# Layer 0 of a four-layer transformer kernel: attention scores by single heads in two row tiles of TensorE, low parts and rotary products on VectorE, and a step of unpacking moved forward

## What is computed

```python
xn = _layernorm(x, axis=-1)
x = x + _L0_attn_ref(xn, ...) + _L0_ffn_ref(xn, ...)
...                                             # layers 1, 2, 3 in the same form

# layer 0, attention: 32 heads of 16 columns
q, k, v = proj(wq), proj(wk), proj(wv)          # (4, 32, 256, 16)
q, k = _apply_rope(q, sin, cos), _apply_rope(k, sin, cos)
scores = einsum('bnth,bnsh->bnts', q, k) / sqrt(16)
scores = where(causal, scores, -inf)
out = einsum('bnts,bnsh->bnth', softmax(scores), v)

# layer 0, FFN: 4-bit weights, W[k, n] = scales[g_idx[k], n] * (w4[k, n] - (z4[g_idx[k], n] + 1))
out = (silu(xf @ Wg) * (xf @ Wu)) @ Wd          # 512 -> 1376 -> 512
```

## Time and profile before

| | |
|---|---|
| median of 3 runs | 2557.12 us (2554.77 to 2557.39) |
| profiled execution, its own time | 2561.34 us |
| span from its first to its last instruction | 2559.6 us |
| mean granted TensorE clock | 0.983 of full speed |
| busy: PE / PEld / DVE | 2455.2 / 1962.8 / 1618.1 us |
| busy: ACT / POOL | 1102.4 / 618.3 us |
| first scores matmul of `att0` to last values matmul | 337.6 to 480.3 us |

### The profile page before, as it was taken

How to read it: one execution, slowest core, us unless ns; L and a number is a source line. 1 busy time by engine, 2 the same in 40 slices (tenths; PEclk the granted TensorE clock), 3 DMA queues, 4 the chain that set the end, 5 groups by cost and what they waited for, 6 DMA issues and landing times. The chain is left out here.

```text
span 2559.6 us, 40914 instructions
## 1 busy us (share of the span) xinstructions
PE 2455.2 (96%) x14448; PEld 1962.8 (77%) x14448; DVE 1618.1 (63%) x2388; ACT 1102.4 (43%) x2158; POOL 618.3 (24%) x455
## 2 busy tenths in 40 slices
PE   5989999999989989999999999999999999999899
PEld 4767777778866668888888878888888877888666
DVE  5886567864477776545444467777777776543576
ACT  3322145443255533223333366666666653323453
POOL 3343110246321226124444400000000024430100
PEclk8999999999989999999999999999999999999999
DMA  2232164122332212234444332222222222322421
GB/s 86 62 101 83 52 122 88 31 38 43 57 89 59 48 28 42 45 98 140 148 148 143 125 114 87 83 90 90 68 75 86 66 44 39 53 46 33 102 63 37
DMA packets 406207, 195.33 MB, mean 76 GB/s; under 512 B 280393, under 2 KB 359729, under 8 KB 406079
## 3 DMA queue, kind: packets, MB, share of 16 engines
q1 hardware_dynamic: 404860, 191.53, 30.0%
q10 hardware_dynamic: 1218, 2.06, 0.3%
HBM read 129.85 MB, written 44.04 MB: 68 GB/s over the span
## 5 line engine op out<-in xcount | busy, mean ns | idle before, releaser
L603 PE MATMUL banks<-xn_hi,w_hi 128*128 128x512 f32 x1264 | 496.6, 393 | 12.9 <-ACT sgf L1146 10.0
L603 PE MATMUL banks<-xn_lo,w_hi 128*128 128x512 f32 x1264 | 493.1, 390 | 0.0
L603 PE MATMUL banks<-xn_hi,w_lo 128*128 128x512 f32 x1264 | 492.9, 390 | 0.0
L603 PEld LDWEIGHTS banks<-xn_hi,w_hi 128*128 128x128 f32 x1264 | 238.0, 188 | 64.4 <-DVE w_lo L591 10.4
L603 PEld LDWEIGHTS banks<-xn_hi,w_lo 128*128 128x128 f32 x1264 | 237.9, 188 | 49.7
L603 PEld LDWEIGHTS banks<-xn_lo,w_hi 128*128 128x128 f32 x1264 | 238.1, 188 | 48.4
L591 DVE TENSOR_TENSOR w_lo<-tw,w_hi 128x512 fp32r<-128x512 f32 (+2 forms) x136 | 117.0, 867 | 201.8 <-ACT w_hi L583 201.7
L2719 DVE TENSOR_SCALAR raw<-banks,cols 128x512 f32<-128x512 f32 x128 | 103.7, 810 | 180.3 <-ACT sq L2702 180.3
L2731 POOL TENSOR_TENSOR ssq<-ssq,sq 128x512 f32<-128x512 f32 x128 | 165.1, 1290 | 183.2 <-ACT sq L2702 183.2
L469 POOL TENSOR_TENSOR nat<-nat,wscale 128x512 f32<-128x512 f32 (+1 forms) x44 | 51.5, 1179 | 651.6 <-DMA nat<-in_L_ffn_w 651.4
L1258 POOL TENSOR_TENSOR h_lo<-sgf,h_hi 128x512 fp32r<-128x512 f32 (+1 forms) x94 | 128.1, 1367 | 288.8 <-ACT h_hi L1149 288.8
(11 more groups left out here) (302 smaller groups left out, 5831.5 us busy)
## 6 DMA issues: line engine op xcount, KB each, us to landing
qk_scratch<-raw SPq DMA_DIRECT2D x64, 512.0 KB, 3.0
qk_raw<-qk_scratch SPq DMA_DIRECT2D x64, 512.0 KB, 3.8
nat<-in_L_ffn_w SPq DMA_DIRECT2D x48, 256.0 KB
head_scratch<-stage SPq DMA_DIRECT2D x16, 512.0 KB, 3.2
st_qs<-st_hi SPq DMA_DIRECT2D x128, 64.0 KB, 2.1
nat<-in_L_attn_Wq SPq DMA_DIRECT2D x32, 256.0 KB
nat<-in_L_attn_Wk SPq DMA_DIRECT2D x32, 256.0 KB
nat<-in_L_attn_Wv SPq DMA_DIRECT2D x32, 256.0 KB
```

What stands on the lines that cost most here:

```text
L603: mm = nc.tensor.matmul(to[half][:, :], w[0:n, j, k * P:(k + 1) * P], r, start=first and k == 0 and x == 0, stop=last and k == len(rows) - ...
```

## The change

**Attention of layer 0.** A slot's 128 rows become two row tiles of 64, one for each head of a pair: rows 0 to 15, 16 to 31 and 48 to 63 of a tile hold the three terms of one head, rows 32 to 35 its four rows of maxima. Each head of a pair has matmuls of its own with 64 rows, in the row tile e = 0 or 1; a step holds heads of one row tile. `both` issues a step of scores and a step of shifted scores of the other row tile alternately. The masks come from two 64-row blocks (`square`, `row64`), so a step's mask is two bf16 matmuls. New functions `pe_att0`, `dve_att0`, `act_att0`, `sp_att0` stand beside the old ones, which layers 1 and 3 still use. Values are split in two halves with the transposes and two `both` between them. ACT copies the maxima in two instructions of 4 rows instead of one of 32. A unit takes 12 loads instead of 9 for the same bytes, and from the fourth on 2 more that clear the maxima rows. The cleared buffers are the queries (128 rows x 2048) instead of the keys (96 rows x 4096).

```diff
+        def score_heads(part):
+            return (0, part, 0, PAIRS) if part < 2 else (1, part % 2, 2 * (part // 2 - 1), 2)
+        def shift_heads(part):
+            return (0, part % 2, 2 * (part // 2), 2) if part < PAIRS else (1, part % 2, 0, PAIRS)
+        def pe_att0(pe, s):
+            def tile(e, width):
+                return slice(e * ROW_TILE, e * ROW_TILE + width)
+            def both(i, part, j, part2):
...
+                for b in range(2):
+                    if here:
+                        nc.tensor.matmul(o[:, :, qt * P + b * ROW_TILE:qt * P + (b + 1) * ROW_TILE], square[tile(e, ROW_TILE), 0, b, :],
+                                         bcast(row64[tile(e, ROW_TILE), :], n_p), start=b == 0, stop=False, skip_group_check=True)
+                    if there:
+                        nc.tensor.matmul(o2[:, :, b * ROW_TILE:(b + 1) * ROW_TILE], square[tile(e2, ROW_TILE), 1, b, :],
+                                         bcast(row64[tile(e2, ROW_TILE), :], n_p2), start=b == 0, stop=False, skip_group_check=True)
+                for x in range(PAIRS):
+                    if here and x < n_p:
+                        mm = nc.tensor.matmul(o[:, x, :], q[tile(e, ROW_TILE), p + x, qt * P:(qt + 1) * P], k[tile(e, ROW_TILE), p + x, 0:keys],
+                                              start=False, stop=x == n_p - 1, skip_group_check=True)
...
+                    if there and x < n_p2:
+                        mm = nc.tensor.matmul(o2[:, x, :], k2[tile(e2, ROW_TILE), p2_ + x, kb * P:(kb + 1) * P],
+                                              q2[tile(e2, ROW_TILE), p2_ + x, kb * P:SEQ],
+                                              start=False, stop=x == n_p2 - 1, skip_group_check=True)
...
+            for i in range(-3, CHUNKS):
+                for n in range(3):
+                    both(i + 2, 3 + n, i + 1, n)
+                values(i, 0, 0)
+                tops(i + 2)
+                for n in range(2):
+                    both(i + 3, n, i + 1, 3 + n)
+                values(i, 0, 1)
+                values(i, 1, 0)
+                values(i, 1, 1)
+                both(i + 3, 2, i + 1, 5)
...
+        def act_att0(act, s, wo):
+            def copy_tops(i, e):
...
+                rows = slice(e * ROW_TILE + QUAD, e * ROW_TILE + QUAD + PAIRS)
+                ins = nc.scalar.activation(att_queries(s, i)[rows, :, :], bcast(bank[5][rows, i % 2 * SEQ:(i % 2 + 1) * SEQ], PAIRS), ACT.Copy)
```

```diff
         def dve_low_x(dve, s, half):
-            for k in range(0, KT, 2):
-                low_x(dve, nc.vector, s, half, k)
+            for k in range(KT):
+                low_x(dve, s, half, k)
...
+                nc.vector.tensor_tensor(seqs(v), seqs(v), bcast(cst[:, C_COS0:C_COS0 + SEQ], 2), ALU.mult).then_inc(step_c.sem, 1)
                 nc.vector.tensor_tensor(seqs(rot), seqs(rot), bcast(cst[:, C_SIN0:C_SIN0 + SEQ], 2), ALU.mult)\
```

```diff
             ins.then_inc(dequant.sem, 1)
+            if i + 1 < s.n:
+                dve_unpack(dve, s, i + 1, (i + 1) % SLOTS, parts_of(s, i + 1))
+            dve_lo(dve, s, i, j, parts)
...
+            def down_ahead(left):
+                if left == 1:
+                    dve_unpack(dve, s.then, 0, 0, parts_of(s.then, 0))
+                    dve_dequant(dve, s.then, 0, 0, parts_of(s.then, 0))
```

More of the change, by code:

```diff
@@ L61 @@
 C_MASK = 384
+C_NEG1 = 512
 C_COS0, C_SIN0, C_COS1, C_SIN1 = 520, 776, 1032, 1288
@@ L98, in constants @@
     c[96 + np.arange(HPC), C_NEG + np.arange(HPC)] = -1.0
+    for e in range(2):
+        c[e * ROW_TILE + QUAD + np.arange(HPC // 2), C_NEG1 + np.arange(HPC // 2)] = -1.0
+    row, of, to = np.arange(P)[:, None] % ROW_TILE, np.arange(2)[None, :, None] * ROW_TILE, np.arange(P)[None, None, :]
+    for x, later in enumerate((of + row[:, :, None] > to, to > of + row[:, :, None])):
+        c[:, C_SQUARE + 2 * P * x:C_SQUARE + 2 * P * (x + 1)] = np.where(later, MASKED, 0.0).reshape(P, 2 * P)
+    c[:, C_SQUARE + 4 * P:] = row == np.arange(ROW_TILE)[None]
     for _, row, groups in TABLES:
@@ L1141, in ahead @@
                     pe_up_delta(pe, s, i, j, ft)
-            up_rounds(pe, s, ahead, work, opening, lead=LEAD - 1 if s.behind else LEAD_TURN, first=first, seam=seam_pe(pe, s))
+            def down_ahead(left):
+                if left == 1:
+                    pe_down_ahead(pe, s.then, 0)
+            up_rounds(pe, s, ahead, work, opening, lead=LEAD - 1 if s.behind else LEAD_TURN, first=first,
+                      seam=down_ahead if s.then else seam_pe(pe, s))
         def act_gate(act, s, half):
@@ L1248, in work, with down_ahead @@
                     dve_gated(dve, s, half)
-            up_rounds(dve, s, ahead, work, opening, LEAD if s.tw is None else LEAD_TURN, first, pair, 1, seam_dve(dve, s))
+            def down_ahead(left):
+                if left == 1:
+                    dve_unpack(dve, s.then, 0, 0, parts_of(s.then, 0))
+                    dve_dequant(dve, s.then, 0, 0, parts_of(s.then, 0))
+            up_rounds(dve, s, ahead, work, opening, LEAD if s.tw is None else LEAD_TURN, first, pair, 1,
+                      down_ahead if s.then else seam_dve(dve, s))
         def pool_up_scale(pool, s, i, j, ft):
@@ L1375, in proj_order @@
         def proj_order(s, ahead, work, opening, lead=LEAD, seam=None):
-            for i in range(min(lead, s.n)) if opening else ():
+            for i in range(1 if s.up and s.up.then is s else 0, min(lead, s.n)) if opening else ():
                 ahead(i, i % SLOTS, s.chunks[i])
@@ L1389, in load, with pe_down_ahead @@
             def load(i, j, c):
-                sp_slot(sp, s, i)
+                if s.up and s.up.then is s and i < SLOTS:
+                    sp.wait_ge(centred.sem, s.up.cen0 + s.up.n - (s.up.n - 1 - i) % SLOTS)
+                else:
+                    sp_slot(sp, s, i)
                 for dst, src in c["loads"]:
                     sp.dma_start(dst(j), src).then_inc(loaded[j].sem, 16)
+            if opening and s.up and s.up.then is s:
+                load(0, 0, s.chunks[0])
             proj_order(s, load, lambda i, j, c: None, opening, LEAD_LOAD)
+        def pe_down_ahead(pe, s, i):
+            c = s.chunks[i]
+            pe_spread(pe, s, i, i % SLOTS, [HOT["down"] + kt * P for kt in c["kts"]], c["cols"])
         def pe_chunk_delta(pe, s, i):
@@ L1402, in ahead @@
                 if s.mode == "dequant":
-                    pe_spread(pe, s, i, j, [HOT["down"] + kt * P for kt in c["kts"]], c["cols"])
+                    pe_down_ahead(pe, s, i)
                 elif s.adapters:
@@ L3287, in build @@
         down0 = plan_proj(packed_down_chunks(t["L0_ffn_down_qweight"], F0), "dequant", KT, h_of((h0_hi, h0_lo)), "dve", up0)
+        up0.then = down0
         v0 = plan_v0()
```

291 lines of the change are left out of this document (224 added, 67 removed).

## The result

| | before | after |
|---|---|---|
| median, runs made in turn | 2557.0 us | 2569.16 us |
| ratio, 95% interval | | 1.0045 [1.0034, 1.0056] |
| profiled execution, its own time / span | 2561.3 / 2559.6 | 2569.62 / 2567.8 us |
| first scores of `att0` | 337.6 | 330.0 |
| last values of `att0` | 480.3 | 492.7 |

The change is slower by 0.45%, against 2525 us forecast. By stages of the two profiled executions, the front gains 7.6 us, attention takes 162.7 instead of 142.7 and loses 20, and what lies behind is 4 shorter: 8.2 us of span, as measured. The 4 us are no gain that is shown: in the nine traces whose code behind attention is that of the change, this stretch takes 2071.8 to 2080.7 us (from the end of the last values), and before it took 2079.1.

What follows compares the result with a forecast made beforehand. PE was taken as the bound in attention, DVE in `up0`. From 2561.3 us, attention -14, `up0` -8, seam -5.5 and norms -5 gave 2528.8 profiled, 2525 against the median; range 2515 to 2535, chance 0.47.

Steps and rivals of the forecast that it cites:

- Loads and clears: Attention of layer 0: 12 or 14 loads per unit for the same 1.5 MB and halved clears stay covered; cost 0.
- Score tiles, the period: Attention of layer 0: row tiles side by side, scores and shifts 2.9 us, the period falling from 8.74 to 7.6 us.
- The ring: Attention's dependency loop through PE, ACT and DVE, said to bound the period: 7.3 us, with hand-overs 7.6.
- weight loads queue: Rival, 0.18: in attention, weight loads for the two row tiles go one after the other; ring 8.5 us, time 2538.
- no overlap: Rival, 0.11: row tiles run one after the other in attention; period 10.2 us, time 2564, slower.
- Evacuation: Rival, 0.11: copies out of PSUM on DVE and ACT bound attention; period 6.9 us, attention -25, time 2514.
- Fifteen periods at 1.14: Attention of layer 0: fifteen periods each save 8.74 - 7.6 = 1.14 us, giving 17 us.
- Ramps and adapters, 3 us between 1 and 5: Attention's cost for deeper pipeline filling and draining, the second copy, and adapters' transposes on DVE with less slack.
- `up0`, -8: Up product of layer 0: less DVE work and contention with POOL saves 8 us, between 3 and 12.
- DVE fills up: Rival, 0.13: work moved to DVE takes what vanished contention gives; `up0` gives 1, norms 1, time 2537.
- The seam, -5.5: Between up and down product: with chunk 0 ready, the first product starts near 240.0, not 244.4; 1.3 more from half rate.
- Norms, -5: Norms' low parts on DVE alone: blocks 2 and 3 end earlier, 0.6 us for each of 8 halves; between 0 and -8.

Runs made afterwards that it cites:

- e2_stride: The change with unit loads taking the two row tiles in turn and two row groups per tile on every second row; 2544.1 us, 0.9953 of before.
- e8: Kernel before with only the change's parts ahead of attention, but norms' low parts again shared between VectorE and POOL; 2549.4 us, 0.9968 of before.
- e10: e7_all with the low parts of the norms shared with POOL again as before; 2534.87 us, 0.9912 of the kernel before.
- e7_all: e2_stride plus the adapters' transposes spread one per chunk and the first down chunk loaded early; 2535.73 us, 0.9918 of the kernel before.

## Why the prediction was wrong

The step that failed is this one: "Loads and clears. 12 or 14 loads per unit for the same 1.5 MB lie over 15 us of attention per unit [...] Both stay covered; [...] Cost 0." It counted bytes and loads, and took the rate of before for granted. The rate fell from 203 to 125 GB/s with the place and order of the rows. It also looked at a unit in the steady state, 12.6 us of load per 14.3, and not at the first four units, whose loads stand in one queue with 20 us of wo loads. "Uncovered, a late unit would stop PE once per unit" was the right price to ask for: PE stopped once, for 14 us, and the late queue then delayed the adapters' loads as well. With only the place and order of the rows mended (e2_stride), 1.0045 becomes 0.9953. By the Trainium skill's 104 GB/s ("SBUF — State Buffer", Door 1) a unit takes 15.1 us, my estimate from that page; two periods last 14.3. The prediction didn't weigh it.

A second term was put at nothing without a word: the granted clock. Before, it is 1.00 all through `att0`. With row tiles it is 0.50, the 1.2 GHz level, from 332.2 to 349.3, and in the change again from within or just behind PE's long waits: of 13.9 us (373.2 to 390.2), 3.4 (417.5 to 427.8), 2.9 and 1.9 (455.1 to 465.3) and 2.3 (472.2 to 475.6). The tenth period of the change shows what that costs:

```profile
421.50:431.60 10.10, 9.74 (x127) 7.07 (x123) 5.03 (x9) 5.70 (x9) 0.73 (x1) 0.69 1.01 131
431.60:438.70 7.10, 6.74 (x126) 5.02 (x122) 5.69 (x9) 5.70 (x9) 0.73 (x1) 1.00 0.20 22
```

PE waits there no longer than in the undisturbed one (0.36 us), and the period takes 10.08 us and not 7.16: 2.9 us for a stretch at half clock. DMA traffic doesn't do this: the twelfth period has a DMA share of 0.80 at full clock, and takes 7.16. So a wait of PE costs more than its own length.

Point by point:

- *Score tiles, the period:* the tiles run side by side, and the period is 7.16 us, better than 7.6 and outside the 7.4 to 7.8 that was named as the sign. Scores and shifts cost 3.5 and not 2.9: a short `both` takes 0.49 us (361.78 to 362.27) where a step of that shape took 0.35, the longer ones 0.63 to 0.71 for 0.62. The prediction's other estimate, 3.4 from a speedup of 1.54, came out, though not its period of 8.1; the sentence that the column tiles show no such loss goes wrong: at 0.227 us per 512 columns, eight matmuls of 128 in four tiles would take 0.11 us without a loss, and they take 0.22. The ring has hardly a gap: PE waits 0.4 us per period. The rivals "weight loads queue" (8.5) and "no overlap" (10.2) fall: loads for the two tiles start 0.01 us apart (361.84 and 361.85, 0.18 long). "Evacuation" (6.9) is nearer to 7.16 than the forecast, but DVE is busy 5.9 of 7.16 and ACT 5.4 to 5.7: PE's own 6.8 is the bound.
- *Fifteen periods at 1.14:* the first and the last pair of the transposes of the earlier trace rows start 128.2 us apart, and not 15 x 8.74 = 131.1, because the first and the last take 7.3. So the periods had 2.9 us less to give.
- *Ramps and adapters, 3 us between 1 and 5:* mis-sized. With the loads mended (e2_stride), first scores to first transposes give 0.6, the first two periods lose 0.8, the drain behind the last transposes takes 12.7 and not 9.7, and the last three periods lose 10.2 more. Spreading six transposes takes those three from 31.7 to 25.4 us.
- *`up0`, -8:* the last up matmul is at 232.3 and not 238.8: -6.5. Eight pairs take 102.6 us (109.55 to 212.19), against 101 forecast and 108.85. "DVE fills up" falls here; its 2537 should have added up to 2536.
- *The seam, -5.5:* -1.5, and the half clock is still behind it (0.53 from 236.4 to 240.0). The step "with chunk 0 ready" failed: its load stands behind copies that SP's queue waits for until 225.5. SP's queue was passed here too, and was not counted.
- *Norms, -5:* nothing that the medians show (e8, e10). The step that failed is that the blocks would be alone in all eight halves; in three, POOL's sum runs beside the last one. PE's wait stayed at 8.9 us.

With loads, adapters and the seam mended (e7_all), the trace has attention at 127.9 us from first scores to last values, -14.8 against -14 forecast, and 9.5 us ahead of it against 13.5. So the mechanism in PE was right. That the size fits is in part luck: the steady period gave 6.6 us more than forecast, of which 2.9 went for the miscount and 3.6 in the periods at both ends. The 3.2 us behind attention lie within the scatter named above. The sign was set by the queue of loads that feeds PE.

Left open: the two waits of 3.4 and 2.9 us in the ninth and thirteenth period of the change, whose releaser reads "issue". The matmuls that wait (heads on L2379 and L2374) have no wait in the program. At 413.6 and 450.2, as a unit's load is ending, one 16 KB packet of the instruction queue starts, and PE goes on 3.3 us later. That fits an instruction fetch that stood behind full DMA engines, and neither wait is there in e2_stride; but no run tried it alone. Nor did a run try why the clock falls in the ramp in every run with row tiles and not in the ramp before, where PE waits for 0.8 us as well.

## What to carry to other kernels

When a change lays operands into other rows, ask for each load how many rows it spreads over, and which rows its neighbours in the queue hit: the rate of before holds only for the place of before. Then follow the whole queue from the first load to the last, with everything that stands in it; one late load is paid once, but all behind it are late as well. And before work is moved to an engine to shorten it, look at what the engine that is relieved does next: three of eight halves of the norms lost what the other five had gained, because its next operation ran beside the last block. Price a wait of PE with the half clock behind it.

## What the runs showed of the hardware

- Loads of the same number, size and count of rows moved 125, 131, 161 or 197 GB/s with equally busy DMA engines (1.01 to 1.07), by the spacing of rows in a load and by which rows neighbouring loads take. Laying 16 rows two apart costs SP 0.59 us per issue instead of 0.43.
- Matmuls in two row tiles of 64 start 0.02 us apart. Two heads of 256 columns, one in each tile, are followed by the next two after 0.20 us, and one alone by the next after 0.20 too. That doesn't show that their columns stream at the same time, since 512 columns in the full array cost 0.23. Four masks of 128 columns, two in each tile, in 0.08 us (361.78 to 361.86) do: two in one tile alone take 0.10 (331.45 to 331.55), so four one after the other would need 0.20.
- SP can stand at one DMA issue while earlier transfers are still moving, and every later load is late with it: one wo issue took 24 us with the DMA engines full (7.7 in e2_stride), one clear of 32 KB 4.8.
- A low part of 128 x 512 on VectorE takes 0.68 us alone and 1.76 beside POOL's sum, in three of 32 blocks.
- A copy on ACT of 4 rows x 1024 takes 1.02 us, as one of 32 rows x 1024 does.
- Behind waits of PE the granted clock is 0.50, for 3.4 to 17.1 us in the change; a period with no wait of its own took 10.08 us at a mean clock of 0.69 and 7.16 at 1.00.
